# Single transpositions placed between products, activation tables loaded without dummy instructions, two layer norms moved to GpSimd, and a new order of all calls

## What is computed

```python
q, k, v = x @ Wq.T + bq, x @ Wk.T + bk, x @ Wv.T + bv      # self attention, one head
attn = sigmoid(layer_norm(q) @ layer_norm(k).T / 16 - log(S))
x = layernorm(x + (attn @ v @ Wo.T + bo) * layerscale)     # first norm
# cross attention with 16 heads of 16 columns over the 77 context rows, softmax
x = layernorm(x + softmax(qh @ kh.T / 4) @ vh @ dense.T + dense_b)   # second norm
# feed-forward: xr, xk mix each row with the row before it
x = layernorm(x + sigmoid(xr @ W_r) * (relu(xk @ W_k) ** 2 @ W_v))   # third norm
```

## Time and profile before

| quantity | value |
|---|---|
| time, median of 3 runs | 535.18 us (534.74 to 535.26) |
| span of the profiled execution | 531.8 us |
| PE busy | 515.0 us |
| PE weight loads busy | 468.3 us |
| DVE busy | 443.7 us |
| ACT busy | 450.4 us |
| POOL busy | 381.9 us |

### The profile page before, as it was taken

The page is one execution under the profiler, slowest core; times in us unless marked ns, Lnnn a source line. Parts: engine busy times, 40 slices in busy tenths (PEclk is TensorE's granted clock), DMA queues, the critical chain, the costliest instruction groups (busy, mean ns, idle before and its releaser), DMA issues.

```text
span 531.8 us, 12709 instructions
## 1 busy us (share of the span) xinstructions
PE 515.0 (97%) x4530; PEld 468.3 (88%) x4530; DVE 443.7 (83%) x995; ACT 450.4 (85%) x1130; POOL 381.9 (72%) x554
## 2 busy tenths in 40 slices
PE   9999999999999999999999999999999898999994
PEld 6888999898989898989898989999898787899994
DVE  4787868878888879797979797778878888999996
ACT  3765579998989898989898989899999899898965
POOL 1774747676867676767667675767778889897996
PEclk9999999999999999999999999999999999999998
DMA  6410120110010110101010100020511000011122
GB/s 193 128 49 21 38 60 6 42 39 2 14 50 27 35 38 24 42 19 52 12 39 3 39 2 22 21 74 28 166 35 41 2 2 1 22 41 41 41 80 100
DMA packets 23269, 22.50 MB, mean 42 GB/s; under 512 B 1724, under 2 KB 23204, under 8 KB 23205
## 3 DMA queue, kind: packets, MB, share of 16 engines
q1 hardware_dynamic: 22770, 21.35, 12.7%
q10 hardware_dynamic: 434, 0.34, 0.2%
HBM read 14.55 MB, written 6.82 MB: 40 GB/s over the span
## 4 chain that ended last, share of the span: by engine, by line
PE 70%; ACT 12%; DVE 9%; issue 4%; POOL 4%; POOLq 0%; DVEq 0%; ACTq 0%
PE st L298 16%; PE acc L298 14%; PE xb L298 10%; PE proj L298 10%; PE xb L2077 5%; PE xb L2096 5%; ACT p_sb L594 4%; PE xb L2064 4%; DVE xm L1485 3%; ACT L545 2%; PE proj L1973 2%; PE xb L1885 1%; POOL rs L1110 1%; PE st L1893 1%; DVE kkT_lo L1299 1%
## 5 line engine op out<-in xcount | busy, mean ns | idle before, releaser
L594 ACT ACTIVATE p_sb<-xb,neg_mx 128x77 f32<-128x77 f32 x512 | 120.0, 366 | 5.2 <-DVE neg_mx L1412 4.9
L1047 POOL TENSOR_TENSOR fold<-p_sb 128x640 f32<-128x640 f32 x32 | 50.2, 1568 | 75.4 <-ACT p_sb L594 75.1
L1052 POOL TENSOR_TENSOR p_sb<-p_sb,rc 128x1280 f32<-128x1280 f32 x32 | 75.3, 2353 | 23.8 <-DVE rc L1425 23.7
L298 PE MATMUL acc<-vv_hi,aT_hi 128*128 128x256 f32 x256 | 76.6, 299 | 0.0
L545 ACT ACT_TABLE_LOAD x58 | 74.4, 1283 | 1.0
L298 PE MATMUL st<-qkT_hi 128*128 128x256 f32 x256 | 74.8, 292 | 0.0
L298 PE MATMUL st<-qkT_lo,qkT_hi 128*128 128x256 f32 x256 | 72.4, 283 | 0.0
L298 PE MATMUL st<-qkT_hi,qkT_lo 128*128 128x256 f32 x256 | 72.4, 283 | 0.0
L298 PE MATMUL acc<-vv_lo,aT_hi 128*128 128x256 f32 x256 | 72.2, 282 | 0.0
L298 PE MATMUL acc<-vv_hi,aT_lo 128*128 128x256 f32 x256 | 72.2, 282 | 0.0
L1412 DVE TENSOR_REDUCE neg_mx<-xb 128x4 f32<-128x308 f32 x128 | 53.7, 467 | 17.1 <-PE xb L2064 16.7
(11 more groups left out here) (262 smaller groups left out, 1707.9 us busy)
## 6 DMA issues: line engine op xcount, KB each, us to landing
xs<-in_x SPq DMA_DIRECT2D x16, 256.0 KB, 3.0
xraw<-in_xT SPq DMA_DIRECT2D x15, 256.0 KB, 2.9
out_y<-y SPq DMA_DIRECT2D x15, 256.0 KB, 2.1
x_kept<-xs SPq DMA_DIRECT2D x10, 256.0 KB, 2.2
x2s_a<-x_kept SPq DMA_DIRECT2D x2, 512.0 KB, 5.0
x2s_b<-x_kept SPq DMA_DIRECT2D x2, 512.0 KB, 7.1
x2s_c<-x_kept SPq DMA_DIRECT2D x1, 512.0 KB, 3.7
cT<-in_cT SPq DMA_DIRECT2D x1, 308.0 KB, 3.3
```

The costliest lines, as they stand in the source:

```text
L298: mm = pe.matmul(out, s_, m_, start=first and k == 0 and q == 0, stop=last and k == n - 1 and q == 2, skip_group_check=not check)
L594: ex = act.activation(weights(t)[:, h // KH * (H // 2) + KH * n + h % KH, 0:SC], logits[n][:, h * SC:(h + 1) * SC], ACT.Exp, bias=neg_mx[: ...
L1047: pool.tensor_tensor(fold[:].rearrange("p (h k) -> p h k", k=FO), p[:, :, 0:FO], p[:, :, FO:2 * FO], ALU.add).then_inc(fo_pool.sem, 1)
L1052: pool.tensor_tensor(weights(t), weights(t), rc[:, t % 2].rearrange("p (h o) -> p h o", o=1) .to_broadcast([P, H, SP]), ALU.mult).then_inc ...
```

## The change

**Transpositions.** `weights_t`, `tqk`, `x1` and `x2` become generators that issue one transposition each time they are resumed. `split_product` takes such a generator (`beside`) and resumes it after each product; `woven(call, i, *turns)` runs a call with transpositions beside it, `alone` runs transpositions in a row. TensorE has 3995 product calls, of which 576 are transpositions, before and after. Before, the 576 stand in 89 groups of 2 to 16. Afterwards 525 stand alone between two products, the other 51 in six groups of 5 to 14.

**Tables.** `table_for` calls `act.preload_act_table(func)`, which is the load alone. The 59 dummies go; there are 56 table loads instead of 59.

**Norms.** `N1` is 3 and `N2` is 0: eight pairs of the first norm and seven of the second go from ScalarE to GpSimd (30 instructions). Nothing else changes engines.

**Order.** All five lists are new. The counts of all other instructions are the same.

```diff
-N1 = 11
+N1 = 3
 NM = 4
-N2 = 7
+N2 = 0
...
-        def split_product(pe, out, stationary, moving, first=True, last=True, check=True):
+        NONE = iter(())
+
+        def split_product(pe, out, stationary, moving, first=True, last=True, check=True, then=None, beside=NONE):
+
             n = len(stationary)
             for k in range(n):
                 (sh, sl), (mh, ml) = stationary[k], moving[k]
                 for q, (s_, m_) in enumerate(((sh, mh), (sh, ml), (sl, mh))):
                     mm = pe.matmul(out, s_, m_, start=first and k == 0 and q == 0,
                                    stop=last and k == n - 1 and q == 2, skip_group_check=not check)
-            return mm
+                    if then and k == n - 1 and q == 2:
+                        mm.then_inc(then, 1)
+                    next(beside, None)
...
+        def alone(turns):
+
+            for _ in turns:
+                pass
+
+        def woven(call, i, *turns):
+
+            beside = chain(*turns)
+            call(i, beside)
+            alone(beside)
...
                     if loaded[0] != func:
                         loaded[0] = func
-                        w.wait_ge(*consts_pool.at(0))
-                        n = 8 * (next(spares) % NSPARE)
-                        act.activation(spare[:, n:n + 1], nlogs[:], func)
+                        act.preload_act_table(func)
...
-                    at(attend, 4 * r - 18, NS, 9)
-                    at(scores, 4 * r - 15, NS, 13)
-                    at(weights_t, 2 * r - 13, NT, 1, 0)
-                    at(tqk, 2 * r - 1, NT, 13)
-                    at(weights_t, 2 * r - 13, NT, 1, 1)
...
+                    cross_scores(2 * r - 12)
+                    scores(4 * r - 15)
+                    attend(4 * r - 18)
+                    woven(scores, 4 * r - 14, weights_t(2 * r - 13, 0), tqk(2 * r - 1), weights_t(2 * r - 13, 1))
+                    woven(attend, 4 * r - 17, weights_t(2 * r - 13, 2))
+                    mixed(r - 7)
+                    qk(2 * r)
+                    cross_scores(2 * r - 11)
+                    v(r)
+                    attend(4 * r - 16)
+                    scores(4 * r - 13)
+                    woven(dense, r - 7, weights_t(2 * r - 12, 0), tqk(2 * r))
+                    woven(scores, 4 * r - 12, x1(r - 5))
+                    woven(qk, 2 * r + 1, weights_t(2 * r - 12, 1))
+                    woven(query, r - 5, weights_t(2 * r - 12, 2))
+                    attend(4 * r - 15)
 
                 warm_up()
+                on_all_rows(0)
+                on_all_rows(1)
                 first_qk()
-                on_all_rows(0)
                 qk(2)
                 qk(3)
-                on_all_rows(1)
-                qk(4)
-                tqk(0)
                 wvo()
+                woven(qk, 4, tqk(0))
...
                 mixed(13)
+                receptance(0)
                 cross_scores(29)
```

More of the change, by code:

```diff
@@ L1 @@
 from contextlib import ExitStack
-from itertools import count
+from itertools import chain
 import numpy as np
@@ L1178, in _ @@
[L1178 to L1190 removed]
+                v_lo(4)
+                keys_apart(3)
+                residual2(0)
+                pads()
@@ new lines, in _ @@
+                qk_deviation(14)
+                deviation1(2)
+                fold_weights(3)
+                residual2(1)
+                residual1(4)
+                normalise(3)
+                qk_deviation(15)
+                for r in range(6, 13):
+                    round_(r)
+                xt_lo(15)
+                fold_weights(18)
+                residual2(9)
+                normalise(18)
+                deviation1(10)
+                norm1(10)
+                qk_deviation(30)
@@ new lines, in _ @@
+                residual1(12)
+                deviation2(7)
+                v_lo(14)
+                fold_weights(19)
+                normalise(19)
+                deviation2(8)
+                v_lo(15)
+                residual2(10)
+                qk_deviation(31)
+                fold_weights(20)
+                deviation1(11)
+                norm1(11)
+                norm2(7)
+                normalise(20)
+                norm2(8)
+                fold_weights(21)
+                normalise(21)
@@ new lines, in _ @@
+                tqk_lo(15)
+                attended(3)
+                sums(4)
+                stats1(3)
+                mixed_lo(1)
+                reciprocals(4)
+                qk_bias(16)
+                maxima(5, 0)
+                maxima(5, 1)
+                qk_stats(16)
+                maxima(5, 2)
+                maxima(5, 3)
+                v_bias(8)
+                qk_norm(16)
+                stats2(0)
+                for r in range(5, 11):
+                    round_(r)
@@ new lines, in _ @@
+                scores(41)
+                scores(42)
+                woven(attend, 38, weights_t(15, 0), tqk(27), weights_t(15, 1))
+                woven(attend, 39, weights_t(15, 2))
+                mixed(7)
+                qk(28)
+                cross_scores(17)
+                v(14)
+                attend(40)
+                scores(43)
+                woven(dense, 7, weights_t(16, 0), weights_t(16, 1), tqk(28))
+                woven(scores, 44, x1(9))
+                attend(41)
@@ new lines, in _ @@
+                woven(query, 9, weights_t(16, 2))
+                qk(29)
+                cross_scores(18)
+                scores(45)
+                scores(46)
+                woven(attend, 42, weights_t(17, 0), weights_t(17, 1))
+                woven(attend, 43, weights_t(17, 2))
+                mixed(8)
+                woven(scores, 47, tqk(29))
+                cross_scores(19)
+                qk(30)
+                scores(48)
+                woven(v, 15, weights_t(18, 0), weights_t(18, 1))
```

1470 lines of the change are left out of this document (810 added, 660 removed).

## The result

The changed kernel takes 562.0 us (561.5 to 562.5), the one before 535.2 us (534.7 to 535.9): 1.050 times as long (95% interval 1.0486 to 1.0515). I had forecast 530.1. The profiled execution took 562.5 us, with a span of 560.8. In every run that has both, the time is 1.8 us above the span. The 3.4 us that I had added to the span were therefore 1.8 us around it and 1.6 us by which the profiled execution of the kernel before was faster than the median.

The account below looks back on a forecast made before the run. PE (TensorE) was taken as the bound, with no wait worth anything in its rounds. Span 531.8 - 0 - 0.7 - 1.4 - 3.0 = 526.7 us, and 3.4 more for the runs' median: 530.1 us; range 520 to 539.

Parts of the forecast that it names:

- are covered by PE: In the middle rounds ScalarE, VectorE and GpSimd are hidden behind PE, busy without waits worth anything, 25.9 us a round.
- Single transpositions: 525 transpositions between two products cost 0.109 us each, as in a group: 0 us; bounds 7.9 us gain, 5.3 loss.
- The rounds did change in length: Sign in the middle rounds: the forecast is wrong if they leave 25.9 us at all.
- The rival of a cheap lone transposition: Transpositions between products cost 0.05 us less each, 504 us in all, or 515 by the skill's figure; chance 0.08.
- the one of a dear switch: A transposition among products pays over 0.01 us for switching on PE: 536 to 545 us; chance 0.08.
- Tables: Dropping 58 dummies and three loads, 11.8 us of ScalarE for the dummies, gains 0 in the rounds; end counted elsewhere.
- Norms: 30 norm instructions, 17.6 us, go to GpSimd, which gets to some 21 of 25.9 us a round: 0.
- My rival on a late first norm: In the rounds, GpSimd's first norm comes over 1.4 us later and holds `x1`; at 2.4 us, 540 us; chance 0.15.
- The start: Bias products behind the warm-up, between a gain of 1.6 us and a loss of 0.9; taken as a gain of 0.7.
- the clock rises soon after 5 us: At the start, PE's clock was expected to rise then, so 0.7 us of gain was taken, nearer the 1.6 bound.
- `cross_scores(29)`: In the end, `receptance(0)`, 1.44 us, placed ahead of this call fills its 1.54 us wait for `oT_lo`: a gain of 1.4.
- The rest of the end: Of the other 12.2 us that PE lost in the end, a quarter comes back: a gain of 3.0, bounds 0 and 8.

Follow-up runs that it names:

- the new end behind the old start: Kernel before up to the steps of tile 24 on every engine, the rest in the changed kernel's order, norms and tables as before: 552.1 us, ratio 1.0321.
- the 25 waits: Changed kernel with 25 more waits on GpSimd, so wide instructions that held up a VectorE instruction start only after it: 551.2 us, ratio 1.0292.
- the moved block: Kernel before with the twelve products of `receptance(0)` put between `mixed(13)` and `cross_scores(29)`: 536.0 us, ratio 1.0022.
- two calls earlier: Kernel before with `cross_scores(26)` moved ahead of `scores(61)` and `cross_scores(28)` ahead of `attend(61)`: 537.3 us, ratio 1.0048.

## Why the prediction was wrong

**The step that failed above all** is that I priced the new lists for TensorE alone. That the other engines "are covered by PE" held in the rounds (3.7 us over seven of them). For the stretches in which the rounds fill and empty the sum has no term for VectorE and GpSimd, without a reason given. The runs showed VectorE held up by GpSimd in 47 places, and 10.8 us of the 26.8 came back when most of these were taken away. The parts, one by one:

**Single transpositions: 0 us, right as the price of one.** The round has 0.23 us for a product and a transposition. Over 28 pairs of a round it is 0.003 us more than in a row, an estimate of 1.6 us for all 525, a third of the loss that I had allowed. The rounds did change in length, which I had named as a sign of being wrong: they last 26.2 to 26.6 us instead of 25.9. The pairs account for 0.1 of it, and the rest isn't assigned; in rows the new order's rounds are longer still (26.6). The rival of a cheap lone transposition fell, and so did the one of a dear switch. The old order with weaving showed a cost that I had not weighed: the last of the twelve comes 1.4 us later.

**Tables: 0, right** (0.4 us, not told from nothing). **Norms: 0, right** in the old order (a loss of 0.9 us). My rival on a late first norm did not come about: no wait of TensorE for `xs` in the middle.

**The start: forecast a gain of 0.7, measured a loss of 0.6 in the median and 3.8 at tile 0 in the profiled execution.** The step that failed is "the clock rises soon after 5 us". With the bias products in front it did so in four of eight traces, and in three of them it fell once more; in the other four it rose at 13.0 to 14.3 us. The 0.6 us that I had read as waits for inputs were the clock as well: in the old trace no idle time stands there, and the first products begin 0.57 and 0.43 us apart, the next ones 0.23.

**`cross_scores(29)`: forecast a gain of 1.4, measured a loss of 1.2 alone, and nothing in the executions without the half clock.** The wait did go, as I said. I had not asked what the twelve products had covered in their old place.

**The rest of the end: forecast a gain of 3.0, measured a loss of 6 to 7 (6.8 with the new end behind the old start).** I summed TensorE's work between landmarks and took three fewer microseconds behind tile 31 as a gain. Measured are 84.6 us from `cross_scores(31)` to the last product, where it was 84.4, with 3.7 us less work in it. I had noted that tile 30 has only 9.5 us of work over a way of 12.2, and called it one place of several. I now think that this cover, at each tile, decides the end; no run shows it.

**The term that was missing: 10.8 us.** I carried the durations of VectorE's and GpSimd's instructions over from the old trace as if they were constants. They depend on each other's place. The old trace had shown it, in rows that I did not use: its 64 `aT_lo` instructions have a mean of 767 ns though most last 0.68, and one reads

```profile
347.34 1.37 DVE L1299 TENSOR_TENSOR aT_lo<-a_sb,aT_hi 128x512 fp32r<-128x512 f32 x1
```

beside a GpSimd instruction that began 0.47 us ahead of it. The old lists have nine such meetings that hold up a VectorE instruction with both inputs in SBUF by over 0.3 us, the new ones 47 (counted in both timelines).

**Sum.** Of the 26.8 us, 10.8 are the meetings (shown by the 25 waits, with the clock that they cost), about 7 the new end (6.8 behind the old start; 5 to 6 of it behind tile 26, with either start), 0.6 to 3.8 the start, some 1.6 the lone transpositions (by their spacing alone). The remaining 3 to 7 us lie between tiles 0 and 24, in waits that the 25 courtesy waits made or left, and are not assigned. Why the new end is worse is argued from its lack of cover and a part of GpSimd's; no kernel that I ran mended it, and it stays open. No variant beat the kernel before.

## What to carry to other kernels

When a change writes all lists anew, price it on every engine, and look first in the old trace for instructions of one form that last differently from place to place: they name pairs of engines that exclude each other, and such pairs meet anew in each order. Before counting a removed wait as a gain, list what stood behind it as cover for somebody else. Before two halves of lists are said not to fit, look at the seam: here one wait of 3.17 us and the half clock behind it hid that the old end was the better one behind either start. No small move improved the order that had been tuned by hand: one block and two calls of its end, moved, cost 1.2 and 2.4 us.

## What the runs showed of the hardware

**VectorE and GpSimd exclude each other for some instructions.** In the changed kernel, VectorE instructions that started at least 0.5 us before the end of a GpSimd instruction of over 1 us, against the others of the same form (median us, worked out from both timelines):

| VectorE instruction | operands | met: count, us | else |
|---|---|---|---|
| `aT_lo<-a_sb,aT_hi` | both in SBUF | 29, 1.97 | 0.68 |
| `qk_sb<-qk_sb,rs` | both in SBUF | 14, 1.38 | 0.69 |
| `xmT_lo<-xm,xmT_hi` | both in SBUF | 6, 1.40 | 0.68 |
| `qkT_lo<-proj,qkT_hi` | one in PSUM | 17, 0.68 | 0.68 |
| `xs<-acc,xs` | one in PSUM | 12, 0.69 | 0.68 |
| `sm<-fold` | one, in SBUF | 11, 0.79 | 0.81 |
| `pT<-xb` | one, in PSUM | 31, 0.69 | 0.68 |

In the table only the tensor-by-tensor instructions with both inputs in SBUF are held up, and they end a fixed time after the other is done: of the 45 instructions of these forms and of `qk_sb<-qk_sb,nb` that last over 1 us, 44 end 0.55 us behind the end of a GpSimd instruction, the last one 0.40. In the middle of the changed kernel a whole scaling passes first; VectorE's timeline

```profile
210.50 2.49 DVE L1442 TENSOR_TENSOR aT_lo<-a_sb,aT_hi 128x512 fp32r<-128x512 f32 x1
```

and GpSimd's timeline beside it

```profile
210.11 2.33 POOL L1149 TENSOR_TENSOR p_sb<-p_sb,rc 128x1280 f32<-128x1280 f32 x1 [0.44 <-DVE rc L1568]
```

GpSimd is held up likewise when it comes second: the `vv_lo` instruction at 86.80, behind VectorE's multiplication, lasts 1.71 us, others 1.28. Such waits are in the 20 us by which GpSimd's busy time rose beyond the work it was given; I didn't count their share.

The meeting with the scaling recurs in every round, and no wait of TensorE for `aT_lo` over 0.1 us is recorded there: `attend` comes late enough. The Trainium skill (SBUF — State Buffer, Who interferes with whom) says that a VectorE instruction with two SBUF inputs contends with a GpSimd instruction that reads SBUF, and that the one that comes first holds the shared ports to its end. The traces agree in every row of the table, and it is the rule that speaks against this change and that the prediction should have weighed.

**The clock's rise at the start is not the same in each execution** when single-row products stand behind the warm-up: four of them took 1.98 or 3.78 us.

**Half clock stood beside waits of TensorE.** In the traces of this case nine waits were 2.85 to 9.12 us long, and a stretch of 3.4 to 10.2 us at a granted clock of 0.50 stands beside each of the nine. Of the waits of 1.4 to 1.8 us some had such a stretch of 3.4 us or more beside them (1.77 at 429 us in the kernel before with the moved block, 1.75 at 416 in the one with two calls earlier), and others had none (1.54 at 424 in the kernel before, 1.72 at 400 in the changed one). A product costs twice as much in it: 0.43 us for a product and a transposition behind the pause at 89 us, 0.23 elsewhere.
